# A GpSimd scatter train that follows the first attention without a barrier, a key-bias sum on VectorE, and one gathered add per batch in the second attention

## The reference

```python
x = x + jnp.tanh(g_xattn[0]) * L0_xattn(layernorm(x), ctx, mask)   # first attention
x = x + jnp.tanh(g_ffn[0])   * L0_ffn(layernorm(x))                # routing, experts
x = x + jnp.tanh(g_xattn[1]) * L1_xattn(layernorm(x), ctx, ctx)    # second attention

# L0_xattn, one head:
Q = query @ Wq.T + bq;  K = ctx @ Wk.T + bk
attn = softmax(where(padding_mask, -inf, Q @ K.T));  out = (attn @ ctx) @ Wo.T + bo

# L0_ffn, 3584 tokens, 8 experts, 2 per token, 1024 places per expert:
w_topk, e_topk = top_k(softmax(x @ Wr), 2)
pos = running count of the token's expert;  keep = pos < 1024
buf[e, pos] = x;  h = rms(buf) * norm_w
buf_out = (gelu(h @ Wg) * (h @ Wu)) @ Wd + buf
combined = x + sum over the two of w_topk * buf_out[e, pos] * keep
fout = (gelu(rms(x) @ fWg) * (rms(x) @ fWu)) @ fWd + x
out = where(either choice was not kept, fout, combined)
```

## Time and profile before

| | |
|---|---|
| time, median of 3 runs | 3170.21 us (3169.03 to 3174.54) |
| the profiled execution's own time | 3169.83 us |
| its span in the profile | 3167.6 us |
| mean granted TensorE clock | 0.971 |
| busy share of the span: PE, VectorE, ScalarE, GpSimd | 95%, 63%, 46%, 20% |
| first attention | 0 to 234.5 us |
| routing stage | 234.5 to 305.9 us |
| experts | 305.9 to 663 us |
| second attention | 663 to 855 us |

### The profile page before, as it was taken

How to read it: one execution, slowest core, us unless ns; L and a number is a source line. 1 busy time by engine, 2 the same in 40 slices (tenths; PEclk the granted TensorE clock), 3 DMA queues, 4 the chain that set the end, 5 groups by cost and what they waited for, 6 DMA issues and landing times. The chain is left out here.

```text
span 3167.6 us, 61097 instructions
## 1 busy us (share of the span) xinstructions
PE 3009.9 (95%) x23464; PEld 2307.8 (73%) x23464; DVE 2008.1 (63%) x4346; ACT 1457.1 (46%) x2845; POOL 626.6 (20%) x903
## 2 busy tenths in 40 slices
PE   8987999989999999999999999799999999889999
PEld 7874566567789999999999999566666667556544
DVE  4664111146577877788787877566666666668664
ACT  3431111125545555555555555466666666546100
POOL 3565000044100221023012200221212112035100
PEclk9998999999899999999999999899999999989999
DMA  9643223257400000000000000100000000239000
GB/s 276 184 139 119 80 100 120 73 172 217 153 1 2 1 2 2 1 1 2 2 1 2 2 2 1 31 16 21 21 16 21 16 21 16 76 104 273 19 17 20
DMA packets 79535, 185.46 MB, mean 59 GB/s; under 512 B 12981, under 2 KB 23202, under 8 KB 78916
## 3 DMA queue, kind: packets, MB, share of 16 engines
q1 hardware_dynamic: 62708, 141.50, 14.2%
q10 hardware_dynamic: 10208, 25.30, 2.7%
q0 software_dynamic: 6336, 14.76, 1.6%
HBM read 150.26 MB, written 27.79 MB: 56 GB/s over the span
## 5 line engine op out<-in xcount | busy, mean ns | idle before, releaser
L2815 ACT ACTIVATE probs<-probs,neg_top 112x375 f32<-112x375 f32 x512 | 281.8, 599 | 16.3 <-DVE neg_top L2738 15.1
L2738 DVE CUSTOM_DVE_ANT_0 probs<-ps,add 112x375 f32<-112x375 f32 x512 | 250.2, 546 | 58.8 <-PE ps L2889 55.1
L2295 DVE TENSOR_REDUCE top<-ps 112x16 f32<-112x1792 f32 x96 | 194.3, 2024 | 58.3 <-PE ps L2533 56.8
L2916 PE MATMUL ps<-ident,probs 112*125 112x112 f32 x1536 | 222.5, 281 | 2.8 <-DVE probs_t L2745 2.8
L2745 DVE COPY probs_t<-ps 125x336 f32<-125x336 f32 x256 | 129.0, 504 | 151.3 <-PE ps L2916 151.3
L1675 DVE TENSOR_TENSOR hidden<-gated,ps 128x512 f32<-128x512 f32 x64 | 44.0, 688 | 285.0 <-PE ps L1718 285.0
L2916 PEld LDWEIGHTS ps<-ident,probs 112*125 112x125 f32 x1536 | 189.7, 188 | 30.7 <-issue 20.2
L3355 PE MATMUL ps<-we,xn_t 128*128 128x512 f32 x448 | 202.7, 616 | 1.5 <-PEq L836 0.9
L2311 DVE TENSOR_TENSOR probs<-probs,inv_sum 112x1792 f32<-112x1792 f32 x96 | 197.2, 2054 | 3.3
L2307 DVE TENSOR_REDUCE row_sum<-probs 112x16 f32<-112x1792 f32 x96 | 193.9, 2020 | 4.3 <-ACT probs L2419 4.3
L2299 DVE TENSOR_TENSOR probs<-ps,top 112x1792 f32<-112x1792 f32 x96 | 194.3, 2024 | 3.3
(11 more groups left out here) (453 smaller groups left out, 6368.9 us busy)
## 6 DMA issues: line engine op xcount, KB each, us to landing
ctx_t<-in_ctx_T_dram SPq DMA_DIRECT2D x96, 375.0 KB, 5.8
ctx_sb<-in_ctx_dram ACTq DMA_DIRECT2D x64, 384.0 KB, 7.7
ctx_sb<-in_ctx_dram SPq DMA_DIRECT2D x32, 384.0 KB, 6.5
...
```

What stands on the lines that cost most here:

```text
L2295: dve.tensor_reduce(top[:, :, :], scores, AX.X, ALU.max).then_inc(s["top_done"], 1)
L2738: dve.tensor_tensor_reduce(out=probs[:, u, h, :], in0=k.ps[0:S, SCORE + h, 0:L], in1=add[:, j % 2, :], scale=1.0, scalar=BIG, op0=ALU.add, ...
L2815: act.activation(probs[:, u, h, :], probs[:, u, h, :], ACT.Exp, bias=neg_top[:, u, h:h + 1], scale=-1.0).then_inc(s["probs_done"], 1)
L2916: mm = pe.transpose(k.ps[0:KR, PT + h % 2, r * S:(r + 1) * S], probs[:, n % 3, h, r * KR:(r + 1) * KR], k.ident[0:S, 0:S])
```

## The change

**A, key-bias sum.** The one-column products of L198 become two of 256 columns, with bk broadcast to 112 rows, so that the 256 values stand in each of 112 partitions; VectorE copies 112 x 256 instead of 128 x 2. In the batches, L551 and `copy_qbk` are gone. VectorE has `query_bias` instead, one pass over 112 x 256 with a running sum, behind the norm of batch j+4. PE no longer waits for VectorE's copy.

**B, routing in first attention's block.** `route_tokens` and its block are gone. Its parts are functions that are called at the end of first attention's own streams, with semaphore waits where the barrier was. GpSimd's scatters wait for landing after every four. `token_half_scales(6)` stands behind four of the last eight scatters of group 1 and their landing. The weights of expert 0 are loaded at j = 24 of the first attention, those of experts 1 and 2 in `run_experts` behind the second load of rows. The order of VectorE and PE in this part is changed.

**C, second attention.** START is 6, and one gathered add follows per batch. `norm_scale` is called for each batch, two gathers later. A weight product is given in two halves, one per batch for j from 0 to 23.

```diff
@@ first attention, opening
-        for c in range(DC):
-            pe.matmul(k.ps[:, o.COLUMNS, 8 + a:9 + a], o.wq[:, c, cut], o.bk[:, c:c + 1], start=c == 0, stop=c == DC - 1)
+    for c in range(DC):
+        mm = pe.matmul(k.ps[0:S, o.BIAS, D:2 * D], o.bk[:, c:c + 1].broadcast_to([P, S]), o.wq[:, c, :], start=c == 0, stop=c == DC - 1)
@@ GpSimd, masks
-                    pool.wait_ge(s["qbk_copied"], j + 1)
+                    pool.wait_ge(s["qbk_done"], j + 1)
@@ GpSimd, behind the loop
-                token_half_scales(k, m, pool, 6)
-                for j in range(B, B + 4):
-                    pool.wait_ge(s["residual_done"], j - LAG)
-                    scatter(j)
-                for g in range(2):
-                    pool.wait_ge(t.scattered[g], 16 * G * TOP_K)
+                scatter(B)
+                scatter(B + 1)
+                pool.wait_ge(t.scattered[1], 16 * 12)
+                token_half_scales(k, m, pool, GH * LAST)
+                scatter(B + 2)
+                scatter(B + 3)
+                pool.wait_ge(t.scattered[1], 16 * 16)
+                shared_scatters(k, m, t, pool)
@@ VectorE
-                def copy_qbk(j):
-                    dve.wait_ge(s["q_copied"], j + 1)
-                    dve.tensor_scalar(qbk[:, j:j + 1], k.ps[0:S, Q, QBK:QBK + 1], w.bqbk[:, :], None, ALU.add).then_inc(s["qbk_copied"], 1)
+                def query_bias(j):
+                    if j >= 2:
+                        dve.wait_ge(s["qbk_done"], j - 1)
+                    dve.tensor_tensor_reduce(out=weighted[:, j % 2, :], in0=xn[:, j % XR, :], in1=w.wqk, scale=1.0, scalar=w.bqbk[:, :],
+                                             op0=ALU.mult, op1=ALU.add, accum_out=qbk[:, j:j + 1]).then_inc(s["qbk_done"], 1)
...
                     if j + XR < B:
                         norm(j + XR)
+                        dve.wait_ge(s["normed"], j + XR + 1)
+                        query_bias(j + XR)
@@ PE, project_q
                         pe.wait_ge(s["q_copied"], j)
-                        pe.wait_ge(s["qbk_copied"], j)
...
-                    for c in range(DC):
-                        mm = pe.matmul(k.ps[0:S, Q, QBK:QBK + 1], xn_t[:, u, c, :], w.wqk[:, c:c + 1], start=c == 0, stop=c == DC - 1)
@@ SP, first attention
+                    if j == 2 * NB + E:
+                        load_expert(k, m, sp, 0)
@@ new function (its four fellows shared_storage, shared_vectors, shared_scalars and shared_products take over the streams of route_tokens)
+def shared_scatters(k, w, t, pool):
+
+    token_half_scales(k, w, pool, GH * (LAST + 1) - 1)
+    for g in (LAST - 1, LAST):
+        for n in range(G * TOP_K):
+            token_scatter(k, t, pool, g, n)
+            if g == LAST - 1 and n == 3:
+                token_sizes(k, w, pool, LAST)
+            elif g == LAST - 1 and n == 7:
+                token_inverses(k, w, pool, LAST)
+            if n % 4 == 3:
+                pool.wait_ge(t.scattered[g], 16 * (n + 1))
+    for g in range(LAST + 1):
+        pool.wait_ge(t.scattered[g], 16 * G * TOP_K)
@@ VectorE's routing steps, in the new order
+    hide(0)
+    token_rows(k, w, t, dve, LAST - 1, PLACES)
+    for x in range(B - HB, B):
+        token_norm(k, w, t, dve, x)
+    token_gains(k, w, t, dve, LAST - 1)
+    hide(1)
+    add_shared(0)
+    token_shift(k, w, t, dve, LAST, q.LOGITS)
+    token_pick(k, w, t, dve, LAST)
+    hide(2)
+    add_shared(1)
+    token_rows(k, w, t, dve, LAST, PLACES)
+    hide(3)
+    add_shared(2)
+    hide(4)
+    add_selves(LAST - 1)
+    token_gains(k, w, t, dve, LAST)
+    add_shared(3)
...
@@ SP, run_experts
+                    if u == 1:
+                        for e in range(1, EXPERT_RING):
+                            load_expert(k, w, sp, e)
@@ second attention
-    START, ADD_LEAD, SCALE_LAG = 4, 10, 3
+    START, SCALE_LAG = 6, 2
...
-                    while ready < min(START + 2 * (j + 1), j + ADD_LEAD, B):
-                        add_fetched(ready)
-                        statistics(ready)
-                        ready += 1
+                    if j + START < B:
+                        add_fetched(j + START)
+                        statistics(j + START)
...
-                    if 3 <= j < 3 + PRODUCTS - FIRST:
-                        multiply_weights(j - 3 + FIRST)
+                    if j < HALVES:
+                        multiply_half(j // DC + FIRST, j % DC)
```

414 lines of the change are left out of this document (205 added, 209 removed).

## The result

| | before | changed |
|---|---|---|
| median | 3169.86 us (3169.03 to 3174.54, 4 runs) | 3126.68 us (3120.5 to 3132.15, 4 runs) |
| ratio, 95% interval | | 0.986 [0.9839, 0.9882] |
| the profiled execution's own time, span | 3169.83, 3167.6 us | 3132.15, 3130.3 us |

The changed kernel is 43.2 us faster. The forecast was 3131.3 with a range of 3121 to 3146, so it held, and its central value is 4.6 us off. Its parts were off by more than that, and in both directions. The profiled execution of the changed kernel is the slowest of its four, so the two spans differ by 37.3 us. This table has the marks by which the time is followed; each is the start of an instruction in the two traces.

The account below looks back on a forecast made before the run. PE was taken to bound first attention, and PE and VectorE alternate stretches of second attention. Gains of 11.9 (A), 12.5 (B) and 14.5 (C), 38.9 us, off 3169.83 gave 3130.9, predicted as a 3131.3 us median, range 3121 to 3146.

Parts of the forecast that it names:

- Part A, the product term: First attention: PE loses its one-column products, 0.38 us in each of 26 batches, 9.9 us, bounds 8.3 to 12.9.
- Part A, the early stall: First attention at 32.28 us: PE's 3.46 us wait for `copy_qbk` goes, worth 2.0 us, between 1 and 3.
- Part A, VectorE's share: First attention: the sum takes 0.6 us, VectorE gains 0.4 per batch, and 5.0 of 5.6 us stays under PE.
- The rival that VectorE becomes the bound: First attention: contention with GpSimd fills VectorE's 5.6 us per batch, A gives some 2 us, total 3141.2; chance 0.12.
- Part B, the boundary: First attention to routing: without the barrier, group 2's scatters start 5 us earlier, at 236.1 instead of 241.06.
- the price of the scales behind four scatters: Boundary: VectorE's token norms, and everything behind them on VectorE, come 6.5 us later.
- Part B, the trains and the end of the block: Routing: group 2 takes 27.1 us, group 3 25.9, the block end 4.1; the block ends 12.7 us earlier.
- A landing wait: GpSimd's scatters: each wait costs 1.5 us, ten of them 15 us.
- Part B, the reading of the late signals: Routing: unbroken trains of indirect DMAs delay signals; pauses after every four let them through, so 14.53 us idle go.
- Part C: Second attention: 24 half-product batches at 4.53 us, loop 142.2 instead of 158.8, 16.6 less; 14.5 us taken.
- The late start of 2.1 us: Second attention: six adds ahead of the loop, two more than before, start it 2.1 us later.

Follow-up runs that it names:

- run 5: Changed kernel with PE's two one-column products per batch put back, result unused, beside VectorE's sum: 3131.25 us; kernel before beside it 3145.67.
- the second pair: Later traces of the kernel before and the changed kernel, unedited, on one chip: 3169.31 and 3127.31 us, ratio 0.9867.
- run 4: Changed kernel with the statistics of batches 8 to 11 given one or two batches later: 3125.74 us.
- run 6: Changed kernel with part A undone, one-column products on PE and VectorE's copy back: 3139.65 us, 0.9976 of the kernel before.
- run 3: Changed kernel with `token_half_scales(6)` moved ahead of the four scatters, where the kernel before had it: 3127.35 us.
- before_again: The kernel before, unedited, traced again on the third set's chip: 3169.31 us.
- combined: The kernel of run 12, all single edits together: 3130.12 us.
- run 12: Changed kernel without landing waits, scales, sizes and inverses early, statistics later, copies ahead of second attention's masks: 3130.12 us.
- run 1: Changed kernel with all ten landing waits taken out: 3119.9 us, 0.9903 of the kernel before.
- run 11: Changed kernel with ScalarE's copies of second attention's first weight products ahead of its two mask steps: 3133.13 us.
- after_again: The changed kernel, unedited, traced again on the third set's chip: 3127.31 us, 0.9867 of the kernel before.

## Why the prediction held, and where its steps failed

**Part A, the product term: right.** Forecast 0.38 us a batch, measured 0.40 in the changed kernel and, put back, in run 5. The trace disagrees with the rule of the Trainium skill, TensorE: Matmul & The Clock Gate, section Back-to-back issue gap, if its floor for a single matmul is taken alone: that would have made it 0.1 us, and four weight loads with four one-column matmuls cost PE 0.40. The same section says that in a stream of loads and matmuls the two together set the spacing; with that the trace agrees, at 0.10 us a pair.

**Part A, the early stall: wrong.** "This wait of PE goes", worth 2.0 us. It went, and the scores of batch 3 came only 0.6 us earlier (1.7 in the second pair). VectorE stands before the same x, now for 2.84 and 1.66 us, and the x lands nearly when it did before: the wait ends at 30.75, before at 31.38. PE had run ahead by 7 us and lost it all; its next instruction waits until 33.84. The step should have asked at which time the loads land, not how long a wait lasts. Run 4 shows that the order of the statistics was the cause.

**Part A, VectorE's share: partly right.** The rival that VectorE becomes the bound holds nowhere over a stretch, but at one batch: where the choice of experts and the place sums of group 0 stand (129.5 us), the interval is 9.9 instead of 7.8 us. Some 0.5 of these 2.1 us go with VectorE's work, which makes PE wait 0.74 us, and 1.6 with the lower clock behind that wait (run 4). The forecast had no term for the clock. The sum's 32 passes take 0.48 to 0.85 us, 0.57 on average, and 0.08 for its second instruction, close to the 0.6 of the forecast. The Trainium skill, SBUF — State Buffer, section Who interferes with whom, has VectorE instructions with two SBUF inputs contend with GpSimd instructions that read SBUF: the trace agrees, as the pass of 0.85 us at 34.90 lies beside GpSimd's add at 34.73 and its mask at 35.45, and that of 0.48 at 32.25 beside none. Part A gave 7.8 and 9.4 us at the last scores and 8.9 by run 6, where 11.9 were forecast; the term that failed is the 2.0 us of the early wait, and most of the rest is the interval at the place sums.

**Part B, the boundary: right.** From the last scores to the first scatter of group 2 it gained 4.6 us (4.7 in the second pair); the forecast was 5. That includes the price of the scales behind four scatters. VectorE waited 5.35 us for them, and run 3 shows 5.2 us more to be had.

**Part B, the trains and the end of the block: mis-sized.** From the first scatter of group 2 to the experts 57.1 us were forecast (27.1 + 25.9 + 4.1), and the changed kernel takes 64.4, where the kernel before took 65.4. That is where part B's missing 7 us are. A landing wait, taken at 1.5 us in addition to the issue gap, costs 2.06. The Trainium skill, DMA: Bandwidth & Descriptors, section Anatomy of one DMA — SWDGE (gpsimd) path, gives such a transfer a fixed cost of about 2.0 us, mostly its completion, and the trace agrees. With the small steps and some longer issues, the two trains take 28.9 and 29.2 us instead of 27.1 and 25.9. The experts start 8.63 us behind the start of GpSimd's last idle time, where 1.5 + 4.1 were forecast. Of that, GpSimd's drain takes 5.29 us. The rows of the block's end in the changed kernel, and of the two block ends of the kernel before:

```profile
L259 POOLq DRAIN  x1: 5291/5291/5291, 286.3 to 286.3; - x1
```

```profile
L253 POOLq DRAIN  x1: 2677/2677/2677, 230.8 to 230.8; - x1
```

```profile
L1435 POOLq DRAIN  x1: 2668/2668/2668, 298.3 to 298.3; - x1
```

The two drains of 2.7 us became one of 5.3. The first was saved at the boundary and came back at the end. The sum had taken the 4.1 us of a block with 32 scatters for one with 64. Together part B gave 5.5 us at the experts (13.3 less 7.8; 5.6 in the second pair), where 12.5 were forecast.

**Part B, the reading of the late signals: not shown.** The idle time between the groups went, as forecast, but the runs don't show that the pauses let the signals through. For it: with an unbroken train of group 2 engines stand late in before, before_again and combined, and in the ten traces with pauses none does. Against it as a proof: in these ten the step that stood late before waits 9.2 to 13.7 us for the inverse norms, so a late signal of PE would hide behind that wait; instructions that wait for no semaphore stand as well (run 12); and unbroken trains in run 1 and in group 3 of run 12 delay nothing. A run that keeps run 12's order and adds only the pauses would have told. What is shown is the price: the change trades 14.5 to 15.8 us of idle time for eight waits of 2.06, which is about even, and taking the waits out again makes the stretch shorter by 8.0 us where nothing stands late (run 1) and by 1.4 where something does (run 12, which has the inverse norms ahead of the train as well).

**Part C: right for the loop, with luck in the rest.** Batches with a half took 4.53 us as forecast, and VectorE fits in. The loop took 141.5 and 137.8 us for a forecast of 142.2. The late start of 2.1 us didn't come out as a term of its own: the first mask step comes 37.5 to 45.0 us behind the experts' last product, with the clock of PE (run 11). From the experts' last product to the last mask step, part C gave 17.6 and 10.6 us for a forecast of 14.5; the difference between the pairs is mostly the kernel before, which took 196.6 and 190.9 us.

**What was forecast as nothing.** Behind second attention, in code that is the same in all kernels, the changed kernel gains another 6.2 and 9.3 us. In the first pair 3.3 us of it are in the third attention (from 2015.1 to 2736.6 before, 1984.1 to 2702.3 changed), and this is 721.5 and 721.7 us in the two traces of the kernel before, 719.8 in after_again, and 718.1 to 718.3 in the eleven others. The traces show where they are. In both traces of the kernel before VectorE stands nine times in that layer, every second batch, for 0.31 to 0.33 us in front of the same step, for nothing that the profile shows, and PE's waits for VectorE's residual add up to 10.7 us. In the twelve others it never does, and PE's waits are 7.5 us. One of the nine places in the kernel before, and the same place in the changed one:

```profile
2333.45 0.55 DVE L2738 CUSTOM_DVE_ANT_0 probs<-ps,add 112x375 f32<-112x375 f32 x1 [0.33 <-issue]
```

```profile
2300.87 0.55 DVE L2785 CUSTOM_DVE_ANT_0 probs<-ps,add 112x375 f32<-112x375 f32 x1
```

It stays away when part A or a piece of part C is undone, so it isn't theirs. What makes VectorE stand there is open; no run was made for it.

The rest varies from execution to execution, in either kernel. The last attention takes 124.5 to 132.5 us in the fourteen traces, and gives 2.1 us of the gain in the first pair and 6.6 in the second. The largest step of this kind is one of PE's clock; it is nearly alike within both pairs (0.0 and 0.8 us), but not between other traces. The feed-forward layer behind the third attention takes either 77.2 to 77.3 us (ten traces) or 68.1 to 69.0 (four), in either kernel. In all fourteen PE waits there once for 3.8 us and its clock falls. In the four it is back after 6 to 8 us, in the ten after some 24. Windows of the changed kernel, 5 and 10 us behind the wait, and of the changed kernel again, 10 us behind it:

```profile
2747.00:2752.00 5.00, 5.00 (x12) 2.62 (x11) 2.62 (x5) 1.61 (x3) 0.00 (x0) 0.50 0.01 3
2752.00:2757.00 5.00, 5.00 (x14) 3.14 (x12) 1.29 (x3) 0.87 (x2) 0.00 (x0) 0.50 0.00 0
```

```profile
2753.00:2758.00 5.00, 5.00 (x22) 2.81 (x20) 4.21 (x8) 2.25 (x4) 0.00 (x0) 1.00 0.00 0
```

Steps of 9 us of this kind, from one execution to the next, are as large as most effects here.

So the sum came out right because errors cancelled. At the experts parts A and B together gave 13.3 us, 15.0 in the second pair, for a forecast of 24.4. Against these 9 to 11 us too much stood 6.2 and 9.3 us in code that nobody touched, and in the first pair 3.1 from part C, which gave 3.9 less than forecast in the second.
